# Token attention: the denominators of the softmax from sums of two neighbouring key blocks

## The chip, the cores and the metric

The kernel runs on one core of a Trainium2 chip. The metric is device time in microseconds (us) from one execution of the whole program; several runs are made and their median is used. The engines are named as in the profile: PE is TensorE (PEld its weight loads), DVE is VectorE, ACT is ScalarE, POOL is GpSimd, SP is SyncE with its DMA queue.

## What is computed

The program is a chain of three layers on a tensor of 4 images, 256 channels, 32 by 32 pixels: a convolutional attention, a block of token attention with a gated feed-forward layer, and a mixture of experts, with norms between them. The change is in the second layer alone. There each of the 4 batches has 1024 tokens, 8 heads of 32 channels, and computes

```
q2 = jnp.sum(q * q, axis=-1)
k2 = jnp.sum(k * k, axis=-1)
qk = jnp.einsum('bhqd,bhkd->bhqk', q, k)
attn = -(q2[..., :, None] + k2[..., None, :] - 2.0 * qk) / math.sqrt(hd)
attn = jnp.where(causal, attn, -jnp.inf)
attn = jax.nn.softmax(attn, axis=-1)
out = jnp.einsum('bhqk,bhkd->bhqd', attn, v)
```

The softmax is taken without subtracting a maximum: the kernel forms exp(score), multiplies it with v for the numerator and with a matrix of ones for the denominator, and divides at the end.

## The kernel before, in words

`token_block` holds the second layer. Each engine has its own program, written out by hand in order, and semaphores link them. For one batch the attention has 4 rounds: (head group 0, first 512 queries), (head group 1, first 512), (head group 0, last 512), (head group 1, last 512). A head group is 4 heads. A round walks over the key blocks of 128 keys that its queries may see: 4 in rounds 0 and 1, 8 in rounds 2 and 3. One round and one key block (kb) are a step; a batch has NS = 24 steps, numbered m. The last 4 key blocks of each round lie on the diagonal, and there only queries from `first_query(m)` on are computed, so that these four steps are 512, 384, 256 and 128 queries wide; the others are 512 wide.

One step has three stages. PE computes the scores of 4 heads in two halves of two heads (`scores`, lines 844 and 847, the second being the mask of a diagonal block), each half in its own pair of PSUM banks. ACT takes exp of each half into `probs` (line 1103), which has two slots, m % 2. PE then runs `weigh` (line 870): the numerator, v times probs, 4 heads side by side in four column groups of the array, and the denominator, ones times probs, in the same way. Both are fp32 and the trace shows 8 matmul records for each of the two. PE's order is scores(m+1), weigh(m), scores(m+2), weigh(m+1) and so on, so each scores call is queued behind the weigh of two steps earlier. A half of the scores waits until ACT has emptied its pair of banks, that is for exp of the same half one step earlier.

DVE's program in the attention (`attention`, line 1411) is a list by step. At kb == 1 of rounds 1 to 3 it runs `normalise` of the round before: a reciprocal of the denominators (line 1507) and a product (line 1509). At kb == 3 it runs `low_part` of the round before (line 1515). In the last round, at key block 5, it runs `statistics` of the next batch (lines 1275 to 1289), and at the last step `norm_factors` (line 1294) and `second_norm` (line 1475). ACT's program (line 1094) has, between the exps: at kb == 2 of rounds 1 to 3, after the exp of that step, `aT` of the round before (line 1153), a copy that waits for `normalise`; two `x_copy` pairs; and after the exp of step 22 `late_roots` and `norm_roots` (lines 1125 and 1036), square roots of which the second waits for `statistics` and which are enclosed by two table loads. All of ACT's and DVE's instructions run strictly in this order. PE's last work of the attention is weigh(23), and then `late` begins with `h2_turned` (line 909), transposes of what `second_norm` wrote.

Batches 0, 1 and 2 each carry such work for the next batch (x_turned, x_copy, statistics, norm_factors); batch 3 does not.

## Time and profile before

| what | value |
| --- | --- |
| median of 3 runs | 1603.47 us (1595.92 to 1610.03) |
| the profiled execution | 1605.05 us |
| span from its first to its last instruction | 1603.3 us |
| mean granted TensorE clock over the span | 0.896 |
| busy over the span | PE 79%, DVE 49%, ACT 44%, POOL 26% |

The span is read as layers in order of time: the first layer until about 350 us, the token block until about 998 us, then routing and experts. The shares of busy time are means over layers with different limits, so the attention's own stretches have to be looked at. In the rows below a granted clock of 1.00 is 2.4 GHz and 0.50 is 1.2 GHz. A row of a timeline can merge several instructions of one line; its duration is then from the first start to the last end. The end of a matmul is modelled and overlaps the start of the next one.

### The profile page before, as it was taken

Reading aid. Unit: us, or ns where it says so; the run is one execution under the profiler, and the core shown is the slowest. Engines: PE = TensorE matmul, PEld = TensorE weight load, DVE = VectorE, ACT = ScalarE, POOL = GpSimd, SP = SyncE. Lnnn points to the kernel's source line nnn. Section 1 sums busy time; section 2 is a strip of 40 time slices with the busy share of each in tenths; the row PEclk is TensorE's granted clock in tenths of the full one; section 3 lists DMA queues with packets and bytes.
Section 4 is the critical chain, followed back from the end, with each engine's and each line's share of the span. In section 5 each row is a group of like instructions: output and inputs, shape, how many; then the busy total and the mean of one; then the engine's idle time right before and its main releaser. Section 6 shows DMA issues by size and latency. Waiting matters only on the chain. (4 is left out here: it accounts for less than half of the span.)

```text
span 1603.3 us, 27663 instructions
## 1 busy us (share of the span) xinstructions
PE 1267.5 (79%) x9241; PEld 905.8 (56%) x9242; DVE 786.6 (49%) x1442; ACT 697.5 (44%) x1314; POOL 412.3 (26%) x307
## 2 busy tenths in 40 slices
PE   4999999956398789779977986622299999999993
PEld 3777777743134433434444334512288888888882
DVE  3857574715545553654366343824054444444441
ACT  3444433315566756666675562311133333333321
POOL 3939393700000000000000000256223332233321
PEclk7999999977699989988998998555599999999996
DMA  5949494920600060025004201997333333333326
GB/s 178 339 140 328 165 326 147 298 92 33 108 12 14 14 132 15 1 46 101 15 1 83 50 1 53 244 273 167 73 51 54 46 49 49 53 53 51 45 38 220
DMA packets 284049, 166.64 MB, mean 104 GB/s; under 512 B 203456, under 2 KB 266176, under 8 KB 283840
## 3 DMA queue, kind: packets, MB, share of 16 engines
q1 hardware_dynamic: 268512, 142.51, 34.5%
q0 software_dynamic: 15456, 23.08, 8.0%
q8 instruction: 47, 0.77, 0.2%
q14 instruction: 34, 0.28, 0.1%
HBM read 38.66 MB, written 83.11 MB: 76 GB/s over the span
## 5 line engine op out<-in xcount | busy, mean ns | idle before, releaser
L2031 PE MATMUL moe_hbank<-moe_xT,l_w1T 128*128 128x256 f16 x1872 | 213.2, 275 | 49.9 <-DMA moe_xT<-rows_scratch 49.9
L2072 ACT ACTIVATE moe_hid<-moe_hbank,moe_b1T 128x256 f32<-128x256 f32 x312 | 130.8, 470 | 267.1 <-PE moe_hbank L2031 267.1
L2031 PEld LDWEIGHTS moe_hbank<-moe_xT,l_w1T 128*128 x1872 | 184.3, 99 | 72.5 <-issue 50.0
L2046 PE MATMUL moe_ybank<-l_w2T,moe_hid_hi 128*128 x1248 | 206.4, 273 | 0.0
L2010 POOL DMA_INDIRECT acc_scratch<-moe_y,moe_meta x78 | 121.9, 1562 | 315.6 <-DVE moe_y L2099 292.5
L1103 ACT ACTIVATE block_probs<-block_bank 128x1024 f32<-128x1024 f32 (+1 forms) x192 | 144.9, 809 | 80.2 <-PE block_bank L847 65.5
L2046 PE MATMUL moe_ybank<-l_w2T,moe_hid_lo 128*128 x624 | 170.1, 273 | 0.0
L2084 DVE TENSOR_SCALAR moe_hid_hi<-moe_hid 128x2048 f16<-128x2048 f32 x39 | 47.8, 1227 | 218.6 <-ACT moe_hid L2072 218.6
L720 POOL COPY block_stack<-block_stack 128x512 f16<-128x512 f16 x16 | 11.2, 700 | 516.7 <-ACT block_stack L1087 516.7
L2046 PEld LDWEIGHTS moe_ybank<-l_w2T,moe_hid_hi 128*128 128x128 f16 x1248 | 122.1, 98 | 14.1
L844 PE MATMUL block_bank<-block_qkT 128*128 128x512 f16 (+3 forms) x384 | 94.9, 336 | 39.3 <-DMA block_qkT<-block_stack 27.9
L363 POOL TENSOR_SCALAR conv_raw<-conv_raw 128x1024 f32<-128x1024 f32 x32 | 95.2, 2975 | 32.7 <-DMA conv_raw<-in_L_ffn_w 32.7
L844 PEld LDWEIGHTS block_bank<-block_qkT 128*128 128x128 f16 x384 | 34.1, 99 | 117.5 <-ACT block_probs L1103 62.8
L2086 DVE SCALAR_TENSOR_TENSOR moe_hid_lo<-moe_hid,moe_hid_hi 128x2048 f16<-128x2048 f32 x39 | 89.4, 2292 | 1.3
L870 PE MATMUL block_bank<-block_probs,block_v 128*32 128x512 f32 (+3 forms) x768 | 85.1, 516 | 5.8 <-ACT block_probs L1103 5.8
L369 POOL TENSOR_TENSOR conv_raw_lo<-conv_raw,conv_raw_hi 128x1024 f16<-128x1024 f32 x32 | 69.0, 2157 | 74.0 <-DMA w_parts<-conv_raw_lo 71.6
L269 PE MATMUL block_bank<-block_qkv,block_hT 128*128 128x256 f16 (+1 forms) x384 | 70.6, 334 | 20.9 <-ACT block_qk L1062 8.3
L870 PE MATMUL block_bank<-block_probs,block_ones 128*32 128x512 f32 (+3 forms) x768 | 81.4, 496 | 0.0
L269 PE MATMUL block_bank<-block_down,block_ff_hi 128*128 128x256 f16 x256 | 51.7, 307 | 24.2 <-DVE block_ff_lo L1491 24.2
L1507 DVE RECIPROCAL block_h<-block_bank 128x512 f32<-128x512 f32 x12 | 40.3, 3357 | 61.5 <-PE block_bank L870 61.3
L474 ACT ACTIVATE conv_pt_hi<-conv_turned 128x1024 fp32r<-128x1024 f32 x32 | 32.9, 1028 | 82.1 <-PE conv_turned L412 82.1
L269 PEld LDWEIGHTS block_bank<-block_qkv,block_hT 128*128 128x128 f16 x384 | 36.0, 99 | 55.7 <-issue 12.2
(348 smaller groups left out, 2611.0 us busy)
## 6 DMA issues: line engine op xcount, KB each, us to landing
rows_scratch<-l_blank SPq DMA_DIRECT2D x32, 1056.0 KB, 7.5
conv_raw<-in_L_ffn_w SPq DMA_DIRECT2D x32, 512.0 KB, 4.9
w_parts<-conv_raw_lo SPq DMA_DIRECT2D x32, 256.0 KB, 3.4
w_parts<-conv_raw_hi SPq DMA_DIRECT2D x32, 256.0 KB, 3.6
l_xs<-in_x SPq DMA_DIRECT2D x8, 512.0 KB, 6.9
x_scratch<-l_xs SPq DMA_DIRECT2D x4, 1024.0 KB, 4.0
block_xin<-x_scratch SPq DMA_DIRECT2D x16, 256.0 KB, 3.1
acc_scratch<-block_res SPq DMA_DIRECT2D x16, 256.0 KB, 2.2
```

The source lines that it names most:

```text
L269: last = pe.matmul(out, a, b, start=start and k == 0, stop=stop and k == n - 1)
L363: pool.tensor_scalar(raw[q][:, :], raw[q][:, :], GAIN, None, ALU.mult).then_inc(raw_scaled, 1)
L369: pool.tensor_tensor(raw_lo[:, :], raw[q][:, :], raw_hi[q][:, :], ALU.subtract).then_inc(raw_lo_done, 1)
L844: last = pe.matmul(bank[:, 2 * (n % 2) + i, q0:512], qkT[:, 1, hh, kb * P:(kb + 1) * P], qkT[:, 0, hh, qh * 512 + q0:(qh + 1) * 512], star ...
L870: last = pe.matmul(out[i * HD:(i + 1) * HD, q0:512], lhs, probs[:, m % 2, i, q0:512], start=kb == 0, stop=kb == last_kb)
L1103: act.activation(probs[:, m % 2, 2 * p:2 * p + 2, q0:512], src, ACT.Exp, scale=SCALE).then_inc(S["exp_done"], 1)
L2010: pool.indirect_dma_start(acc, bass.IndirectOffsetOnAxis(ap=meta[r][:, t, 0:1].bitcast(U32), axis=0), y[r % 2][:, t, :], None, compute_op= ...
L2031: last = pe.matmul(hbank[:, c, :], w1T[:, e, wp, k, c * P:(c + 1) * P], xT[q][:, xp * CC + k, :], start=n == 0, stop=n == 5)
L2046: last = pe.matmul(ybank[q][:, t, :], (hid_hi, hid_lo)[hp][q][:, c, t * P:(t + 1) * P], w2T[:, e, wp, c, :], start=n == 0, stop=n == 3 * H ...
L2072: act.activation(hid[q][:, c, :], hbank[:, c, :], ACT.Gelu, bias=b1T[:, e, c:c + 1], scale=1.0 / (GAIN * GAIN)).then_inc(S["gelu_done"], 1)
L2084: dve.tensor_scalar(hid_hi[q][:, :, :], hid[q][:, :, :], HID_GAIN, None, ALU.mult).then_inc(S["hi_done"], 1)
L2086: dve.scalar_tensor_tensor(hid_lo[q][:, :, :], hid[q][:, :, :], HID_GAIN, hid_hi[q][:, :, :], ALU.mult, ALU.subtract).then_inc(S["lo_done" ...
```

## The change

`probs` gets four slots (m % 4) instead of two. `weigh` keeps only the numerator. Key blocks 2k and 2k+1 of a round form a couple. DVE gets `couple`: once exp of both steps is done and the numerator of the even step has been computed, it adds the probabilities of the odd step onto those of the even step in place, over the columns that the odd step has (4 heads times its width). PE gets `lengths(k)`: the four products with ones on the sum, one set per couple instead of one per step, queued after the numerator of step 2k+2, the first step of the next couple. ACT's exp now waits for the numerator of four steps ago and for the denominator of the couple that used its slot. `normalise` and `last_round` also wait for the denominators. In DVE's list `couple` stands ahead of everything else of its step.

```diff
--- before.py
+++ after.py
@@ -609,6 +609,7 @@
     steps = [(r, kb) for r, (_, qh) in enumerate(rounds) for kb in range(4 * (qh + 1))]
     diagonal = [kb >= 4 * rounds[r][1] for r, kb in steps]
     NR, NS = len(rounds), len(steps)
+    SLOTS, COUPLES = 4, NS // 2
 
 
     O_STEP, X_STEP, ROOT_STEP = steps.index((NR - 2, 4)), steps.index((NR - 1, 2)), NS - 2
@@ -632,7 +633,7 @@
 
         stack = s.sb("stack", [P, 2, 2, 2, H, 4, HD], F16)
         qkT = s.sb("qkT", [P, 2, H, T], F16)
-        probs = s.sb("probs", [P, 2, 4, 512])
+        probs = s.sb("probs", [P, SLOTS, 4, 512])
         ff_hi, ff_lo = s.sb("ff_hi", [P, FC, 512], F16), s.sb("ff_lo", [P, FC, 512], F16)
         n1, n2 = s.sb("n1", [P, D]), s.sb("n2", [P, D])
         later, barrier = s.sb("later", [P, P], F16), s.sb("barrier", [P, P], F16)
@@ -666,7 +667,7 @@
                  "w_full", "w_hi", "w_lo", "half_inv", "half_attn", "half_hi", "half_lo", "consts", "xin0", "xin1", "norm_loaded", "x_full", "x_copied", "stats_done", "front_scal", "front_act", "late_scal", "late_act", "res_done", "u_done", "h_done",
                  "hsq_done", "h_full", "hT_hi", "hT_lo", "qkv_full", "qk_copied", "v_copied", "gsq_done", "fac_done",
                  "scaled", "squared", "summed", "stack_hi", "stack_dup", "stack_lo", "stack_x", "turned0", "turned1",
-                 "score_full", "exp_done", "av_step", "inv_done", "attn_done", "aT_hi", "aT_lo",
+                 "score_full", "exp_done", "av_step", "coupled", "den_done", "inv_done", "attn_done", "aT_hi", "aT_lo",
                  "o_full", "x2_done", "x2sq_done", "h2_done", "h2_full", "h2T_hi", "h2T_lo", "gate_full", "silu_done", "ffprod_done",
                  "ff_hi_done", "ff_lo_done", "down_full", "o_added", "t2_done", "t2_stored", "log_done", "alpha_done", "passed")
         S = {n: s.sem(n) for n in names}
@@ -862,14 +863,24 @@
                             pe.wait_ge(S["attn_done"], b * NR + (r - 1))
                         if kb == 0 and r == NR - 1:
                             pe.wait_ge(S["o_added"], b * PAIRS + 2)
-                        num, den = bank[:, 4 + 2 * (r % 2), :], bank[:, 5 + 2 * (r % 2), :]
-                        for out, own in ((num, True), (den, False)):
-                            for i in range(4):
-                                hh = 4 * hg + i
-                                lhs = v[:, kb, hh * HD:(hh + 1) * HD] if own else ones[:, :]
-                                last = pe.matmul(out[i * HD:(i + 1) * HD, q0:512], lhs, probs[:, m % 2, i, q0:512],
-                                                 start=kb == 0, stop=kb == last_kb)
+                        num = bank[:, 4 + 2 * (r % 2), :]
+                        for i in range(4):
+                            hh = 4 * hg + i
+                            last = pe.matmul(num[i * HD:(i + 1) * HD, q0:512], v[:, kb, hh * HD:(hh + 1) * HD], probs[:, m % SLOTS, i, q0:512],
+                                             start=kb == 0, stop=kb == last_kb)
                         last.then_inc(S["av_step"], 1)
+
+                    def lengths(k):
+
+                        m = 2 * k
+                        r, kb = steps[m]
+                        q0 = first_query(m)
+                        den = bank[:, 5 + 2 * (r % 2), :]
+                        pe.wait_ge(S["coupled"], b * COUPLES + k + 1)
+                        for i in range(4):
+                            last = pe.matmul(den[i * HD:(i + 1) * HD, q0:512], ones[:, :], probs[:, m % SLOTS, i, q0:512],
+                                             start=kb == 0, stop=kb == 4 * (rounds[r][1] + 1) - 2)
+                        last.then_inc(S["den_done"], 1)
 
                     scores(0)
                     for m in range(NS):
@@ -879,12 +890,15 @@
                             x_turned(nb, 0)
                             x_turned(nb, 1)
                         weigh(m)
+                        if m % 2 == 0 and m:
+                            lengths(m // 2 - 1)
                         if m == O_STEP:
                             output(b, 0)
                             output(b, 1)
                         if m == X_STEP + 1 and nb is not None:
                             x_turned(nb, 2)
                             x_turned(nb, 3)
+                    lengths(COUPLES - 1)
 
                 def output(b, pr, nb=None):
                     wh, wl = w["o"]
@@ -1095,12 +1109,13 @@
 
                     for m in range(NS):
                         q0 = first_query(m)
-                        act.wait_ge(S["av_step"], b * NS + max(m - 1, 0))
+                        act.wait_ge(S["av_step"], b * NS + max(m - SLOTS + 1, 0))
+                        act.wait_ge(S["den_done"], b * COUPLES + max((m - SLOTS) // 2 + 1, 0))
                         for p in range(2):
                             n = 2 * m + p
                             act.wait_ge(S["score_full"], b * 2 * NS + n + 1)
                             src = bank[:, 2 * (n % 2):2 * (n % 2) + 2, q0:512]
-                            act.activation(probs[:, m % 2, 2 * p:2 * p + 2, q0:512], src, ACT.Exp, scale=SCALE).then_inc(S["exp_done"], 1)
+                            act.activation(probs[:, m % SLOTS, 2 * p:2 * p + 2, q0:512], src, ACT.Exp, scale=SCALE).then_inc(S["exp_done"], 1)
                         if steps[m][1] == 2 and steps[m][0] > 0:
                             aT(b, steps[m][0] - 1)
                         if nb is not None and m in (X_STEP + 1, X_STEP + 2):
@@ -1411,6 +1426,8 @@
                 def attention(b, nb):
                     for m in range(NS):
                         r, kb = steps[m]
+                        if kb % 2:
+                            couple(b, m // 2)
                         if kb == 1 and r > 0:
                             normalise(b, r - 1)
                         if kb == 3 and r > 0:
@@ -1428,11 +1445,21 @@
                                 norm_factors(nb)
                             second_norm(b, 0)
 
+                def couple(b, k):
+
+                    m = 2 * k
+                    cols = slice(first_query(m + 1), 512)
+                    dve.wait_ge(S["exp_done"], b * 2 * NS + 2 * (m + 2))
+                    dve.wait_ge(S["av_step"], b * NS + m + 1)
+                    both = probs[:, m % SLOTS, :, cols]
+                    dve.tensor_tensor(both, both, probs[:, (m + 1) % SLOTS, :, cols], ALU.add).then_inc(S["coupled"], 1)
+
                 def last_round(b):
 
                     hg, qh = rounds[NR - 1]
                     r = NR - 1
                     dve.wait_ge(S["av_step"], b * NS + NS)
+                    dve.wait_ge(S["den_done"], (b + 1) * COUPLES)
                     for half, (inv_sem, attn_sem) in enumerate((("half_inv", "half_attn"), ("inv_done", "attn_done"))):
                         cols = slice(half * 256, (half + 1) * 256)
                         inv = h[:, 4 + 2 * (r % 2) + half, :]
@@ -1502,6 +1529,7 @@
                     hg, qh = rounds[r]
                     m = max(i for i in range(NS) if steps[i][0] == r)
                     dve.wait_ge(S["av_step"], b * NS + m + 1)
+                    dve.wait_ge(S["den_done"], b * COUPLES + (m + 1) // 2)
                     inv = h[:, 4 + 2 * (r % 2):6 + 2 * (r % 2), :].rearrange("p a b -> p (a b)")
                     num, den = bank[:, 4 + 2 * (r % 2), :], bank[:, 5 + 2 * (r % 2), :]
                     dve.reciprocal(inv, den).then_inc(S["inv_done"], 1)
```

## Rows read from the trace of the kernel before

**Rows 1.** Windows, batches 2 and 3: length, busy PE PEld DVE ACT POOL, clock, DMA
```profile
732.80:798.00 65.20, 61.91 (x579) 24.75 (x576) 25.47 (x44) 44.30 (x67) 0.00 (x0) 0.97 0.18 39
883.50:946.20 62.70, 59.66 (x561) 22.59 (x558) 21.13 (x23) 40.80 (x61) 0.00 (x0) 0.97 0.12 27
```

**Rows 2.** Groups of instructions by line in the attention of batch 2
```profile
L1103 ACT ACTIVATE block_probs<-block_bank 128x1024 f32<-128x1024 f32 (+3 forms) x48 | 36.3, 809 | 19.2 <-PE block_bank L847 15.4 <-PE block_bank L844 3.6
...
L870 PE MATMUL block_bank<-block_probs,block_ones 128*32 128x512 f32 (+3 forms) x192 | 19.9, 486 | 0.0
```

**Rows 3.** Timeline of PE in batch 2: start us, us, engine, line, operation, tiles, count
```profile
748.60 0.83 PE L870 MATMUL block_bank<-block_probs,block_ones 128*32 128x384 f32 x8
...
750.36 0.61 PE L870 MATMUL block_bank<-block_probs,block_ones 128*32 128x256 f32 x8
...
752.12 0.40 PE L870 MATMUL block_bank<-block_probs,block_ones 128*32 128x128 f32 x8
...
756.91 1.06 PE L870 MATMUL block_bank<-block_probs,block_v 128*32 128x512 f32 x8
757.79 1.04 PE L870 MATMUL block_bank<-block_probs,block_ones 128*32 128x512 f32 x8
758.76 1.04 PE L844 MATMUL block_bank<-block_qkT 128*128 128x512 f16 x4
759.73 1.06 PE L870 MATMUL block_bank<-block_probs,block_v 128*32 128x512 f32 x8
797.45 0.43 PE L870 MATMUL block_bank<-block_probs,block_v 128*32 128x128 f32 x8 [1.46 <-ACT block_probs L1103]
```

**Rows 4.** Timeline of ACT in batch 2, columns as in rows 3
```profile
747.71 1.09 ACT L1103 ACTIVATE block_probs<-block_bank 128x512 f32<-128x512 f32 x2 [1.48 <-PE block_bank L847]
...
751.55 3.77 ACT L1103 ACTIVATE block_probs<-block_bank 128x1024 f32<-128x1024 f32 x4 [1.10 <-PE block_bank L844]
756.58 1.94 ACT L1103 ACTIVATE block_probs<-block_bank 128x1024 f32<-128x1024 f32 x2 [1.26 <-PE block_bank L844]
758.40 0.63 ACT L1153 ACTIVATE block_turned_hi<-block_h 128x512 f16<-128x512 f32 x1
...
793.82 1.28 ACT L1125 ACT_TABLE_LOAD   x1
```

**Rows 5.** Timeline of DVE in batch 2
```profile
743.92 3.36 DVE L1507 RECIPROCAL block_h<-block_bank 128x512 f32<-128x512 f32 x1 [12.56 <-PE block_bank L870]
747.31 0.69 DVE L1509 TENSOR_TENSOR block_h<-block_bank,block_h 128x512 f32<-128x512 f32 x1
...
789.75 1.41 DVE L1275 BATCH_NORM_STATS2 block_stats<-block_t 128x6 f32<-128x256 f32 x4 [3.55 <-ACT block_t L1032]
791.29 0.64 DVE L1279 BATCH_NORM_AGGREGATE block_mv<-block_stats 128x2 f32<-128x6 f32 x8
...
792.61 0.17 DVE L1289 TENSOR_SCALAR block_ta<-block_td 128x8 f32<-128x8 f32 x1
795.46 0.25 DVE L1294 RECIPROCAL block_roots<-block_tb 128x16 f32<-128x16 f32 x1 [2.68 <-ACT block_tb L1036]
...
796.06 1.67 DVE L1475 SCALAR_TENSOR_TENSOR block_qk<-block_qk,block_rr,block_n 128x256 f32<-128x256 f32 x4
```

**Rows 6.** Groups of DVE instructions by shape, whole run
```profile
L2086 DVE SCALAR_TENSOR_TENSOR moe_hid_lo<-moe_hid,moe_hid_hi 128x2048 f16<-128x2048 f32 x39 | 89.4, 2292 | 1.3
L2084 DVE TENSOR_SCALAR moe_hid_hi<-moe_hid 128x2048 f16<-128x2048 f32 x39 | 47.8, 1227 | 218.6 <-ACT moe_hid L2072 218.6
...
L1454 DVE TENSOR_TENSOR block_res<-block_t,block_u 128x512 f32<-128x512 f32 x16 | 10.0, 683 | 0.0
```

**Rows 7.** Busy time by stretch at the end of the attention of batch 2, with granted clock
```profile
799.00:803.00 4.00, 2.42 (x13) 1.09 (x12) 3.62 (x5) 1.01 (x3) 0.00 (x0) 1.00 0.00 0
803.40:805.40 2.00, 0.06 (x1) 0.00 (x0) 1.82 (x4) 0.47 (x2) 0.00 (x0) 1.00 0.00 0
805.40:808.70 3.30, 3.24 (x16) 2.32 (x17) 3.30 (x10) 1.83 (x2) 0.00 (x0) 0.51 0.00 0
```

## The prediction

> **What bounds the kernel now.** I read first the page's busy shares, then windows over the attention of single batches, then the timelines of PE, ACT and DVE side by side. In the attention of batch 2 PE is busy 61.9 of 65.2 us and ACT 44.3; in batch 3, without work for a next batch, PE 59.7 of 62.7 [rows 1]. The reader is to see that PE sets the pace while ACT waits for it: 19.2 us of idle time before the exps, all released by PE's scores [rows 2]. DVE is busy only 25.5 us [rows 1], but in lumps: a reciprocal of 3.36 us per round [rows 5].
>
> A full step takes PE 2.82 us, from 756.91 to 759.73: numerator 0.88, denominator 0.97, scores 0.97 [rows 3]. A step costs ACT two exps, 1.94 us [rows 4]. The attention is a loop of three engines with little slack: exp of one half lets PE write that half's next scores, and those let ACT go on. ACT can never be more than one step ahead, whatever the number of probs slots, since the score banks hold one step.
>
> **What the change removes.** The denominators of the odd steps: widths 384 and 128 in rounds 0 and 1, and 512, 512, 384, 128 in rounds 2 and 3. The row of a group lasts 0.07 us longer than the distance to the next (1.04 against 0.97), so I take 0.97, 0.76 and 0.33 for 512, 384 and 128 columns [rows 3]. Of each, 0.09 (0.97 less 0.88) comes with the turn back to scores and stays. Removed are 0.88, 0.67 and 0.24: 2 x 0.91 + 2 x 2.67 = 7.2 us a batch, 28.6 us in all. That is the whole gain, were PE's time all that counts. An odd step then takes PE 1.94 us, no less than ACT's 1.94, and the handover of about 0.25 us comes on top, so about a quarter of the gain goes to ACT even with nothing else late.
>
> **What it adds on DVE.** The widest add has 2048 elements, 4 heads of 512. No row shows that instruction. An fp32 sum of 512 takes 0.68 us, and a two-input instruction of 2048 takes 2.29; four separate sums of 512 would be 2.73, and a one-input instruction of 2048 takes 1.23 [rows 6]. I take the two-input row less the 0.08 by which DVE's records overlap: 2.2 us, and 1.68 and 0.62 for widths 384 and 128. Ends: 1.23 and 2.73. A batch has 4 x 2.2 + 4 x 1.68 + 4 x 0.62 = 18.0 us; DVE then is at 43.5 of 65 us, so it is not the bound by its sum. Before the denominators of an ordinary couple the add is covered: between the exp that frees it and the PE instruction that needs it stand one numerator, one set of scores and one more numerator, 0.88 + 0.97 + 0.88 = 2.73 us, against 2.2 and two handovers. The waits added to ACT on slots of four steps ago come last nowhere; I take nothing for them (ends 0 and 3 us in all, 96 steps at 0.03).
>
> **What it moves, and the new wait.** In DVE's list `couple` of key blocks 0 and 1 stands ahead of `normalise` of the round before. `couple` needs the exps of key block 1, which `normalise` never needed. Before, in round 2, the reciprocal started 0.07 us after the last denominators and its product ended at 756.67, while ACT came to `aT` only at 758.40 [rows 4]. (By rows 5: 3.39 from the reciprocal's start to the product's, plus 0.69.) `normalise` was hidden with 1.8 us to spare. Now it starts after exp of key block 1 plus the add. Behind `normalise` wait ACT's `aT`, behind that the exps of key block 3, and behind them PE's numerator and its next scores.
>
> I laid the three orders beside each other on the clock of batch 2, with the durations above, handovers of 0.12 to 0.15, and exps of 1.94, 1.52, 1.09 and 0.66. The old order laid in this way ends within 0.5 us of the trace everywhere. After / before:
> - Round 1. PE is 1.2 us ahead when it starts. Exp of key block 1 ends at 744.8; add 1.68, reciprocal and product 4.1: 750.6. ACT is at `aT` at 746.9 and waits 3.7. Copy 0.6, first half of exp 0.33: the scores of round 2 start at 751.6 / 750.5, **1.1 late**.
> - Round 2. Exp of key block 1 ends 756.2, add 2.2, 4.1 more: 762.5. ACT waits from 758.8, 3.7 us. Scores of key block 4 start 764.2 / 761.2, **3.0 late**; PE has been idle 2.9 us. The rest of the round gives back 0.5 to 0.7: **2.3 late** at round 3.
> - Round 3. Exp of key block 1 ends 781.3; product 787.6; ACT waits from 783.2, 4.4 us. Scores of key block 4 at 789.4 / 785.3, **4.1 late**; at step 20 3.5 late.
> - End. In the step of key block 5 `couple` stands ahead of `statistics`. Before, half the statistics ran earlier and the rest from 789.75, beside the exps of that step [rows 5]. Now from the end of those exps at 795.8: add 1.7, all the statistics 4.3 (eight records of 0.35, aggregates 0.65, four small ones 0.85) to 801.8, `norm_roots` to 802.1, table load 1.28 [rows 4], last exp 0.66: 804.0. Behind it stands the last add, 0.6, and only then `norm_factors` and `second_norm`, of which the first transposes want half: 1.35. They start at 806.1 / 798.0, and the second pair waits 0.3 again: **8.4 late**.
>
> Batch 3 has no statistics; it is laid out to 6.0 late. Sum 3 x 8.4 + 6.0 = **31.2 us**. With adds at 1.23 us for the widest it comes to 17, at 2.73 to 39. What follows in `late` hangs on these transposes, in all engines, so it all moves on.
>
> **The clock.** The granted clock in this attention is 0.97 on average [rows 1]. A wait of 1.46 us at 797.45 leaves it at 2.4 GHz [rows 3]. After a stretch from 799 with 2.4 of 4.0 us busy and then a stretch of 2.0 us nearly empty it is 0.51, that is 1.2 GHz, for 3.3 us [rows 7]. The new waits of PE are 2.9, 2.9, 2.7 and 5 us, each longer than the 2.0. Laying half clock over the 3.4 us behind each of them costs 3.5 us a batch, 14 in all, less than half of the work since ACT sets the pace there; none costs 0. I take 2.5 a batch, **10 us**, the greater part since each wait exceeds the one that did it.
> The Trainium skill, "TensorE: Matmul & The Clock Gate", section "HAM oscillation — how this bites in real kernels", says that a kernel whose bursts of matmuls are parted by waits finds the clock throttled again at each burst. By that rule the sum would be 1650, by no fall of the clock 1636; the trace agrees for one wait [rows 7].
>
> **The sum.** 1605.05 (the profiled execution, 1603.3 of it span) + 31.2 + 10 = 1646.3. That execution stood 1.6 above the median of the runs shown; the forecast for a median is 1645.
>
> **Rivals.**
> - All new waits bring the clock down: + 31.2 + 14 - 1.6 = 1649. For: rows 7. Against: 1.46 us did not, and the phase of a wait can matter. Chance 0.2.
> - The adds are cheaper than the two-input row, or the engines recover more between the waits: + 17 and 0 to 5 of clock: 1621 to 1626. For: nothing here shows such an add. Against: the reciprocal and product, 4.1 us, stay behind the exps at any price of the add; with adds at nothing I still get + 2. Chance 0.15.
> - Gain eaten but no more: 1595 to 1612. It needs both cheap adds and `statistics` absorbed. Chance 0.06.
> - Faster: PE's 7.2 us a batch come through, 1603.5 - 28.6 x 0.75 = 1582. Its place is the full steps, its price the denominators, and it decides if ACT's `aT` doesn't wait, that is if `normalise` ends before ACT is there. For: PE is at 95% and everything else idles beside it. Against: the lay-out of round 2 misses that by 3.7 us. Chance 0.05.
> - The change doesn't shed the work (denominators as long as before for another reason): the waits without the gain, some 1665. Chance 0.04.
>
> **Chances and range.** The forecast holds 0.5. One per cent, 16 us, is about what can be told from no change. Faster by over 1%: 0.05. Within 1% (1587 to 1619.5): the eaten gain and the lower edge of the cheap adds, 0.08. Slower by over 1%: 0.87. Range: from the cheap adds with little clock, 1621, to adds at 2.73 (+ 39) with all the clock (+ 14), 1655, and a little for the spread of runs: 1620 to 1659.
>
> **What would show it.** In the changed profile: denominators with ones at half the count, 96 records a batch instead of 192, and some 11 us busy instead of 19.9 [rows 2]; an add of 2.1 to 2.3 us at its widest; ACT idle 3 to 4.5 us before each of 12 `aT` copies, released by the product at line 1509's successor; a reciprocal that starts right behind an add instead of behind the denominators; `norm_roots` waiting some 3 us for `statistics` in three batches; the attention of batch 2 some 73 to 77 us long instead of 65.2, of batch 3 68 to 73; half clock behind most of PE's long waits. Wrong would be: `aT` without a wait, PE waiting mainly for the adds of ordinary couples, or a loss that sits behind the attention, in `late`.

## The result, and the profile after

The changed kernel is slower: 1657.09 us, median of 4 runs (1647.68 to 1658.44), against 1603.74 for the kernel before beside it; ratio 1.0323, 95% interval 1.0263 to 1.0382. The profiled execution took 1655.82 us, span 1654.1, 50.8 above the profiled one of before.

First where the time went. The windows below run from the first scores of each batch to the first transposes that follow its attention; the columns are window, length, busy us (instructions) of PE, PEld, DVE, ACT and POOL, granted clock, DMA share, GB/s. Before:

```profile
427.95:496.92 68.97, 64.86 (x584) 25.62 (x585) 28.49 (x51) 46.85 (x71) 0.61 (x1) 0.94 0.24 47
579.07:646.96 67.89, 63.05 (x587) 25.14 (x584) 28.24 (x52) 46.33 (x70) 0.52 (x1) 0.97 0.19 46
731.87:798.03 66.16, 62.87 (x585) 25.32 (x585) 25.47 (x44) 45.22 (x68) 0.00 (x0) 0.97 0.20 42
880.02:946.15 66.13, 61.18 (x571) 23.37 (x568) 23.51 (x31) 43.89 (x64) 0.14 (x1) 0.97 0.18 32
sum 269.15, PE 251.97 PEld 99.45 DVE 105.70 ACT 182.28 POOL 1.28; mean PE 62.99 PEld 24.86 DVE 26.43 ACT 45.57 POOL 0.32
```

After:

```profile
430.58:512.44 81.86, 64.69 (x489) 24.05 (x489) 45.91 (x62) 46.98 (x71) 0.62 (x1) 0.85 0.20 40
595.16:676.37 81.21, 63.40 (x490) 23.70 (x488) 45.10 (x62) 46.13 (x69) 0.00 (x0) 0.88 0.16 39
761.86:841.83 79.97, 63.21 (x488) 23.62 (x489) 42.90 (x55) 45.70 (x68) 0.00 (x0) 0.87 0.16 36
923.76:998.12 74.36, 58.31 (x475) 20.43 (x472) 41.79 (x42) 44.76 (x66) 0.62 (x1) 0.93 0.14 30
sum 317.40, PE 249.60 PEld 91.79 DVE 175.71 ACT 183.58 POOL 1.23; mean PE 62.40 PEld 22.95 DVE 43.93 ACT 45.90 POOL 0.31
```

The attentions are 12.9, 13.3, 13.8 and 8.2 us longer: 317.4 less 269.15 is 48.2 us, nearly all of it. The stretches between them are the same to 0.6 us (579.07 less 496.92 is 82.15, 595.16 less 512.44 is 82.72). Two more readings: DVE's busy time has gone up by 70 us, and PE's has gone down by only 2.4, though a hundred instructions a batch are gone and 28.6 us of work with them. The work that is left has become slower: the clock is 0.85 to 0.93 where it was 0.94 to 0.97.

ACT in batch 2, the copies of line 1168 (1153 before, [rows 4]) and the root of line 1050:

```profile
782.52 0.63 ACT L1168 ACTIVATE block_turned_hi<-block_h 128x512 f16<-128x512 f32 x1 [3.87 <-DVE block_h L1537]
...
795.18 0.63 ACT L1168 ACTIVATE block_turned_hi<-block_h 128x512 f16<-128x512 f32 x1 [3.82 <-DVE block_h L1537]
...
821.51 0.63 ACT L1168 ACTIVATE block_turned_hi<-block_h 128x512 f16<-128x512 f32 x1 [4.60 <-DVE block_h L1537]
...
837.40 0.22 ACT L1050 ACTIVATE block_tb<-block_ta 128x16 f32<-128x16 f32 x1 [2.46 <-DVE block_ta L1304]
```

Each copy now stands behind an idle stretch of 3.8 to 4.6 us, released by the product of `normalise`. [rows 4] show none ahead of the copy at 758.40. DVE at the same places:

```profile
776.74 1.76 DVE L1455 TENSOR_TENSOR block_probs<-block_probs 128x1536 f32<-128x1536 f32 x1 [4.45 <-PE block_bank L869]
778.41 3.35 DVE L1535 RECIPROCAL block_h<-block_bank 128x512 f32<-128x512 f32 x1
...
788.86 2.29 DVE L1455 TENSOR_TENSOR block_probs<-block_probs 128x2048 f32<-128x2048 f32 x1 [1.34 <-ACT block_probs L1118]
791.07 3.35 DVE L1535 RECIPROCAL block_h<-block_bank 128x512 f32<-128x512 f32 x1
...
831.35 1.76 DVE L1455 TENSOR_TENSOR block_probs<-block_probs 128x1536 f32<-128x1536 f32 x1 [3.31 <-ACT block_probs L1118]
833.02 2.70 DVE L1290 BATCH_NORM_STATS2 block_stats<-block_t 128x6 f32<-128x256 f32 x8
...
839.70 0.69 DVE L1455 TENSOR_TENSOR block_probs<-block_probs 128x512 f32<-128x512 f32 x1 [2.34 <-ACT block_probs L1118]
```

The reader is to see the sequence add, reciprocal, with no gap: 2.21 us from the start of the widest add to the next instruction (788.86 to 791.07), and the reciprocal follows the add instead of the denominators [rows 5]. At 831.35 the add is ahead of the statistics, all eight of which then run in one piece, and ACT's root waits 2.46 us for them; at 839.70 the last add is ahead of `norm_factors`. PE's waits of over 2 us in this batch:

```profile
783.48 1.73 PE L845 MATMUL block_bank<-block_qkT 128*128 128x512 f16 x4 [2.85 <-ACT block_probs L1118]
...
796.78 0.39 PE L845 MATMUL block_bank<-block_qkT 128*128 128x512 f16 x1 [2.90 <-ACT block_probs L1118]
...
798.87 1.94 PE L869 MATMUL block_bank<-block_probs,block_v 128*32 128x512 f32 x8
...
821.53 1.76 PE L793 MATMUL block_bank<-all_ident,block_xin 128*128 128x128 f32 x7 [3.84 <-DVE block_h L1537]
...
839.63 0.65 PE L869 MATMUL block_bank<-block_probs,block_v 128*32 128x128 f32 x8 [4.24 <-ACT block_probs L1118]
```

The third of them, at 821.53, is not ahead of scores but ahead of line 793, the transposes of the next batch's input. And the numerator at 798.87, behind the second wait, lasts 1.94 us, where one of that width took 1.06 [rows 3]. The windows before and behind these waits, with the granted clock as the third number from the right:

```profile
783.40:786.80 3.40, 3.32 (x15) 0.98 (x16) 2.98 (x5) 2.24 (x4) 0.00 (x0) 0.54 0.00 0
793.90:796.70 2.80, 0.00 (x0) 0.00 (x0) 1.22 (x2) 1.52 (x3) 0.00 (x0) 1.00 0.00 0
796.70:800.20 3.50, 3.26 (x16) 0.85 (x16) 2.44 (x2) 2.92 (x4) 0.00 (x0) 0.59 0.00 0
817.30:821.50 4.20, 0.39 (x2) 0.00 (x0) 4.17 (x4) 0.00 (x0) 0.00 (x0) 0.97 0.00 0
821.50:824.90 3.40, 3.37 (x19) 1.98 (x23) 0.05 (x1) 3.39 (x5) 0.00 (x0) 0.54 0.25 73
...
839.60:843.10 3.50, 3.00 (x22) 1.60 (x23) 2.71 (x7) 0.12 (x1) 0.00 (x0) 0.50 0.00 0
```

Behind each of the four waits of batch 2 the clock is 0.50 to 0.59, that is 1.2 GHz for most of the 3.4 to 3.5 us that follow. During the second and the third wait, 793.90 to 796.70 and 817.30 to 821.50, it is at 2.4 GHz still (1.00 and 0.97).

Not every new wait does it. The whole attention has 15 of them, four in each of batches 0 to 2 and three in batch 3. Behind 12 the granted clock is 0.50 to 0.63; behind one, of 3.01 us at 945.67, it is 0.77, since it falls only about 2 us later; and behind two, of 2.46 us at 467.49 and 2.52 at 959.23, it stays at 1.00. The first of these two and the one of 3.01 us:

```profile
467.49:470.89 3.40, 3.20 (x24) 1.26 (x24) 2.50 (x2) 2.89 (x4) 0.00 (x0) 1.00 0.00 0
...
945.67:949.07 3.40, 2.99 (x16) 0.69 (x16) 3.24 (x6) 2.54 (x4) 0.00 (x0) 0.77 0.00 0
```

### The profile page after: what moved, and what is told of

Same layout as the page of the kernel before. It is cut to its first block and busy times, and to the rows that moved or that the text cites. A ratio compares the mean times of both kernels' runs of the same rounds, so it can differ in the third digit from the quotient of the medians.

```text
span 1654.1 us, 27098 instructions
## 1 busy us (share of the span) xinstructions
PE 1271.5 (77%) x8857; PEld 901.2 (54%) x8858; DVE 860.9 (52%) x1490; ACT 699.6 (42%) x1314; POOL 412.5 (25%) x307
## 5 line engine op out<-in xcount | busy, mean ns | idle before, releaser
L2112 DVE TENSOR_SCALAR moe_hid_hi<-moe_hid 128x2048 f16<-128x2048 f32 x39 | 47.9, 1228 | 216.7 <-ACT moe_hid L2100 216.7
L845 PE MATMUL block_bank<-block_qkT 128*128 128x512 f16 (+3 forms) x384 | 105.8, 363 | 67.8 <-ACT block_probs L1118 39.2
L1455 DVE TENSOR_TENSOR block_probs<-block_probs 128x1536 f32<-128x1536 f32 (+2 forms) x48 | 75.9, 1581 | 137.5 <-ACT block_probs L1118 75.0
L869 PE MATMUL block_bank<-block_probs,block_v 128*32 128x512 f32 (+3 forms) x768 | 92.9, 559 | 14.3 <-ACT block_probs L1118 14.3
L269 PE MATMUL block_bank<-block_turned_hi,block_gate 128*128 128x512 f16 x128 | 49.0, 426 | 22.2 <-DVE block_probs L1514 16.2
```

Source lines behind the costliest of these rows:

```text
L269: last = pe.matmul(out, a, b, start=start and k == 0, stop=stop and k == n - 1)
L845: last = pe.matmul(bank[:, 2 * (n % 2) + i, q0:512], qkT[:, 1, hh, kb * P:(kb + 1) * P], qkT[:, 0, hh, qh * 512 + q0:(qh + 1) * 512], star ...
L869: last = pe.matmul(num[i * HD:(i + 1) * HD, q0:512], v[:, kb, hh * HD:(hh + 1) * HD], probs[:, m % SLOTS, i, q0:512], start=kb == 0, stop= ...
L1455: dve.tensor_tensor(both, both, probs[:, (m + 1) % SLOTS, :, cols], ALU.add).then_inc(S["coupled"], 1)
```

## The experiments

They ran in later sessions, in which the kernel before takes 1591.4 to 1593.5 us; so ratios to it are compared, and the changed kernel was run there twice:

> The changed kernel itself, beside the others on one chip, as their measure: ratio to before 1.026 to 1.038 as recorded; all differences between variants are read against this run.

Measured: 1637.94, ratio 1.0287 [1.0250, 1.0324]. And once more, with more runs:

> The changed kernel once more beside the busy waits, as their measure: ratio to before 1.025 to 1.035; granted clock 0.85 to 0.89 in the attention of batches 0 to 2.

Measured: 1637.91, ratio 1.0288 [1.0264, 1.0311]. The loss in these sessions is 44 to 47 us, where it was 53 in the first.

**Thin adds.** Is it the adds' time?

```diff
-                    cols = slice(first_query(m + 1), 512)
+                    cols = slice(511, 512)
```

> The changed kernel, with each of the 48 adds cut to one column per head (4 elements); every wait, the order of all engines and the halved denominators stay. Left out of the computation: the probabilities of the odd key blocks in the denominators. Theory A (the adds' time, 18 us a batch, counts because they stand in DVE's queue ahead of the reciprocal, the statistics and the second norm): nearly all of the loss goes, 1600 to 1612 us, and waits of ACT at the copies fall from 3.9-4.6 us to under 2. Rival B (the order alone does it: the reciprocal starts only behind the exps of key block 1, whatever the add costs): at least half of the loss stays, 1630 or more. Rival C (the halved denominators would be a gain if only the adds were free): 1575 to 1590.

Measured: 1602.29, ratio 1.0048 [1.0032, 1.0064]. The loss falls from 44 us to 8 or 9. Theory A holds and B falls, but not all of A is as expected: the copies still wait 27.1 us in 12 times, 2.3 each, where under 2 was expected, since the reciprocal stays behind the exps of key block 1. C falls as well: even free adds leave no gain under this order.

**The order at key block 1.**

```diff
-                        if kb % 2:
-                            couple(b, m // 2)
                         if kb == 1 and r > 0:
                             normalise(b, r - 1)
+                        if kb % 2:
+                            couple(b, m // 2)
```

> The changed kernel with normalise ahead of couple in the step of key block 1. Theory A: the copies of ACT wait 1.2 to 2.6 us instead of 3.9 to 4.6, but PE now waits 1 to 3.4 us for the add that comes behind the reciprocal; the laid-out sum falls from 49 to 35 us over before: 1635 to 1645. Rival D (ACT's wait at the copies is nearly the whole loss, and moving it away frees it): 1615 to 1625. Rival E (the half clock and PE's lack of work behind any stall make it all the same): no change within 5 us of 1656.

Measured: 1624.59, ratio 1.0185 [1.0155, 1.0216], 30 to 32 us above before. The expectation was written against 1604: by ratio A is 1.019 to 1.026 and D 1.007 to 1.013, so the measured one lies at A's lower edge, though 1624.59 as an absolute time would fall into D. The waits moved as expected. Who waited for whom, total us, times, longest:

```profile
DVE block_h L1535 <- PE block_bank L881: 52.7, 12, 5.0
...
PE block_bank L881 <- DVE block_probs L1455: 24.6, 12, 3.3
...
ACT block_turned_hi L1168 <- DVE block_h L1537: 23.8, 12, 2.6
```

The copies wait 23.8 instead of 48.3 us, and 24.6 us of PE waiting for sums have come in their place; 16 us net, by the difference of the ratios. D and E fall. The line at the top shows the third place of a queue: the reciprocal now waits for the denominators of the last, narrow couple, which PE computes only in the step after the round. The 52.7 us are no loss by themselves (the reciprocal waited 61.3 us before the change as well, 10 times); what counts is how late it starts, and that is measured below.

**The order at the end of the attention.**

```diff
-                        if kb % 2:
+                        if kb % 2 and m not in (X_STEP + 3, ROOT_STEP + 1):
                             couple(b, m // 2)
...
                             second_norm(b, 0)
+                        if kb % 2 and m in (X_STEP + 3, ROOT_STEP + 1):
+                            couple(b, m // 2)
```

> The changed kernel with the adds of steps 20/21 behind statistics, and that of steps 22/23 behind norm_factors and second_norm. Theory A: the stretch from step 20 to the first transposes of late gets 3 us shorter in three batches and 1 in the last; with the half clock behind it 8 to 13 us in all: 1643 to 1649. Rival: the end of the attention is not part of it (the statistics only move), 1653 to 1658.

Measured: 1628.67, ratio 1.0217 [1.0182, 1.0253]. By ratio that is about 11 us below the changed kernel, within the 8 to 13 expected; the absolute times of the expectation went by the first session, and as ratios to 1604 they would be 1.024 to 1.028, above the measured one. In the attention the root of line 1050 waited 7.2 us for the statistics in the changed kernel, in 3 times; in this run it doesn't wait for them.

**Both orders.**

> The changed kernel with both moves in DVE's queue: normalise ahead of couple at key block 1, and statistics, norm_factors and second_norm ahead of the couples of their steps. Theory A: the two gains (20 and 16 us) act at different places of a batch and add up, less a little: 15 to 25 us above before, ratio 1.009 to 1.016; what is left are PE's waits for the add behind the reciprocal. Rival (one wait takes the other's place, so the moves don't add): 28 us or more above before.

Measured: 1614.57, ratio 1.0146 [1.0106, 1.0186]: 21 to 23 above before. The single moves took away 16 and 11, both together 22: they add up, less a little, within the uncertainty of 6 to 9 us that each of these differences has. Left over, as expected:

```profile
DVE block_h L1537 <- PE block_bank L881: 52.1, 12, 5.0
...
PE block_bank L881 <- DVE block_probs L1457: 25.7, 13, 3.3
ACT block_turned_hi L1168 <- DVE block_h L1539: 23.8, 12, 2.6
```

**The cost without the gain.**

```diff
+    SINGLE = (0, 1, 2, 3, 4, 5, 6, 7, 8, 9, 10, 11)
...
+                        if m // 2 in SINGLE:
+                            own_lengths(m)
...
-                    dve.tensor_tensor(both, both, probs[:, (m + 1) % SLOTS, :, cols], ALU.add).then_inc(S["coupled"], 1)
+                    dve.tensor_tensor(sums[:, :, cols], both, probs[:, (m + 1) % SLOTS, :, cols], ALU.add).then_inc(S["coupled"], 1)
```

> The changed kernel with the denominators of every step as before (two sets per couple, from the single probabilities) while DVE still does all 48 adds at the same places, into a scratch buffer that nobody reads but whose slots ACT waits for, and each add waits for the one before it. The change's cost without its gain. Theory A: PE has its 7.2 us a batch back, of which the waits hide about half: 10 to 16 us above the changed kernel, that is 4.0% to 4.4% above before. Rival F (the denominators' time is hidden entirely under the new waits): within 4 us of the changed kernel. Rival G (the loss comes from PE waiting for the sums, not from the queue order): near the kernel before, less than 1% above it.

Measured: 1651.09, ratio 1.0358 [1.0323, 1.0393], 13 us above the changed kernel beside it (11 by the ratios). That is within the 10 to 16 us of A, but 3.6% above before and not the 4.0 to 4.4% into which the expectation had translated them. So of the 28.6 us of removed denominators 11 to 13 arrive even there, and 58 us (1651.09 less 1593.47) are what the adds and their waits cost. F and G fall.

**The wait that the lay-out had missed.**

```diff
-                        if m == X_STEP and nb is not None:
+                        if m == X_STEP + 1 and nb is not None:
                             x_turned(nb, 0)
...
-                        if nb is not None and m in (X_STEP + 1, X_STEP + 2):
-                            for pr in (2 * (m - X_STEP) - 2, 2 * (m - X_STEP) - 1):
+                        if nb is not None and m in (X_STEP + 2, X_STEP + 3):
+                            for pr in (2 * (m - X_STEP - 1) - 2, 2 * (m - X_STEP - 1) - 1):
```

> The changed kernel with x_turned and x_copy of the next batch one step later, so that PE doesn't wait for the product of round 2's normalise ahead of the numerator of step 18. That wait (3.8 us of PE in each of three batches) was not in the prediction's lay-out. Theory A: the exps of step 19 stay behind the copy, so only what PE could not do meanwhile comes back: 2 to 4 us below the changed kernel, ratio to before 1.025 to 1.028. Rival (PE's 3.8 us are lost whole): 8 to 12 us below it, 1.021 to 1.023.

Measured: 1631.68, ratio 1.0256 [1.0219, 1.0293] against 1.0287: about 5 us less, but the intervals overlap, and this one reaches into the ranges of both theories. The trace says more: with the transposes out of the way PE's third wait in batch 2 is still 3.56 us, now ahead of the scores of step 20 and for the exps that stand behind the copy. So the 3.84 us were not an extra wait, which speaks for A. The last wait of the batch is 3.09 us where it was 4.24.

**Which pairs are worth adding.** The last two steps of a round are 256 and 128 wide: their pair saves 0.24 us of PE, and holds up the end of the round. Here they have their own denominators, at once:

```diff
+    SINGLE = (1, 3, 7, 11)
+    PAIRED = COUPLES - len(SINGLE)
...
+                        if m // 2 in SINGLE:
+                            own_lengths(m)
...
-                        if kb % 2:
-                            couple(b, m // 2)
                         if kb == 1 and r > 0:
                             normalise(b, r - 1)
+                        if kb % 2 and m // 2 not in SINGLE and m not in (X_STEP + 3, ROOT_STEP + 1):
+                            couple(b, m // 2)
...
                             second_norm(b, 0)
+                        if kb % 2 and m // 2 not in SINGLE and m in (X_STEP + 3, ROOT_STEP + 1):
+                            couple(b, m // 2)
```

> Both moves in DVE's queue, and the last couple of each round (widths 256 and 128) is not added: its two steps have their own denominators, at once behind their numerators, so that the round's denominators are complete in its last step and the reciprocal starts as early as before the change. Eight couples of twelve are left, whose removed denominators are 0.67, 0.88 and 0.88 and 0.67 us. Theory A: ACT's copies wait no more, PE waits only about 1 us for the first sum of rounds 2 and 3: 10 to 18 us below before, ratio 0.989 to 0.994. Rival (any add in DVE's queue costs more than its denominators give): at or above before.

Measured: 1573.80, ratio 0.9887 [0.9842, 0.9932]: faster than before by 18 us, and than the changed kernel by 64. Against the kernel with both orders and all twelve pairs it is 41 us faster (1614.57 less 1573.80): that is what the four narrow pairs of each batch cost there. Who waited for whom:

```profile
DVE block_h L1554 <- PE block_bank L881: 34.0, 12, 4.6
...
PE block_bank L894 <- DVE block_probs L1474: 2.7, 4, 0.7
```

No line of a copy waiting for `normalise` is left; PE waits 2.7 us in all for sums. DVE and then ACT in the second and third key block of round 2 in batch 2:

```profile
743.80 3.36 DVE L1554 RECIPROCAL block_h<-block_bank 128x512 f32<-128x512 f32 x1 [0.16 <-PE block_bank L881]
747.19 0.69 DVE L1556 TENSOR_TENSOR block_h<-block_bank,block_h 128x512 f32<-128x512 f32 x1
747.80 2.28 DVE L1474 TENSOR_TENSOR block_probs<-block_probs 128x2048 f32<-128x2048 f32 x1
751.33 2.29 DVE L1474 TENSOR_TENSOR block_probs<-block_probs 128x2048 f32<-128x2048 f32 x1 [1.25 <-ACT block_probs L1135]
```

```profile
746.93 1.94 ACT L1135 ACTIVATE block_probs<-block_bank 128x1024 f32<-128x1024 f32 x2 [0.40 <-PE block_bank L847]
748.75 0.63 ACT L1185 ACTIVATE block_turned_hi<-block_h 128x512 f16<-128x512 f32 x1
```

The order is reciprocal, product, add; the product ends at 747.88, the copy at 748.75 doesn't wait, and the widest add, still 2.28 us, falls into time in which DVE has nothing else to do. What the narrow pair did can be read from the start of the reciprocal, against the first exp of the round it stands in (round 2 of batch 2). With both orders and all pairs it starts 4.1 us after it (769.95, the exp at 765.85). With the wide pairs it is 1.0 (743.80 and 742.76), as before the change (752.59 and, in [rows 4], 751.55):

```profile
752.59 3.36 DVE L1507 RECIPROCAL block_h<-block_bank 128x512 f32<-128x512 f32 x1 [0.15 <-PE block_bank L870]
```

The same pairs with DVE's old order:

> The wide pairs alone, eight couples, but with DVE's queue in the changed kernel's order: couple ahead of normalise, statistics and second_norm. Theory A: the order is what costs, so this stays near the changed kernel, 1.024 to 1.034 of before; the copies of ACT still wait 3.5 us and more, 12 times. Rival (the four narrow couples cost the time, since their sums hold up the end of each round): most of the loss goes, below 1.010.

Measured: 1641.09, ratio 1.0306 [1.0274, 1.0339], and

```profile
ACT block_turned_hi L1185 <- DVE block_h L1554: 51.6, 12, 4.6
```

4.3 us a copy. The choice of pairs alone gives nothing (1.0306 against 1.0287), the order alone takes away half of the loss (1.0146), and only both together make a gain (0.9887). And with two pairs fewer; the edit sets `SINGLE = (1, 2, 3, 7, 8, 11)`, and couples 2 and 8 are the first of rounds 1 and 3, not of 1 and 2 as the expectation says:

> As the wide pairs with both moves (eight couples), and two couples fewer: the first couples of rounds 1 and 2, whose adds stand behind the reciprocal, have their own denominators again. Six couples of twelve are left. Theory A: what PE waits for those two sums is worth about what their denominators cost, so the time is that of the eight-couple kernel within 4 us, 0.985 to 0.992 of before. Rival (fewer adds, less gain, in proportion): 4 to 8 us above the eight-couple kernel, 0.991 to 0.994.

Measured: 1578.54, ratio 0.9893 [0.9854, 0.9932], the same as with eight pairs as far as can be told. The denominators of the two pairs are 0.67 and 0.88 us, 6.2 in all four batches; the uncertainty of the difference between the two runs is some 9 us, and the interval reaches into the rival's range. That an add right behind a reciprocal gives nothing and costs nothing is therefore not shown, only that two such pairs don't matter by more than this.

**The clock by itself.** PE is kept at work where it waits, with products whose weights are nought:

```diff
+                    def keep_busy(m, sets):
+
+                        num = bank[:, 4 + 2 * (steps[m][0] % 2), :]
+                        for _ in range(sets):
+                            for i in range(4):
+                                pe.matmul(num[i * HD:(i + 1) * HD, :], nought[:, :], v[:, 0:2, :].rearrange("p t d -> p (t d)"), start=False, stop=False)
...
                         if m == X_STEP and nb is not None:
+                            keep_busy(m, 4)
...
                             lengths(m // 2 - 1)
+                            if m in (6, 10) or (m == X_STEP and nb is None):
+                                keep_busy(m, 3)
+                            if m == ROOT_STEP and nb is not None:
+                                keep_busy(m, 4)
```

> The changed kernel with extra products on PE where it waits: weights of nought onto the numerator's bank, so that nothing changes in what is computed. Three sets of 4 (about 0.88 us a set) in round 1 and in round 2 ahead of the late scores, four ahead of x_turned in round 3, four ahead of the last numerator (in the last batch three in round 3 and none at the end). ACT's and DVE's orders and waits stay. Theory A (the half clock behind PE's waits costs 10 us and more beside the waits themselves): the granted clock in the attention rises from 0.87 to 0.95 or more, and the time falls by 8 to 16 us below the changed kernel. Rival H (the clock's fall is hidden under ACT's and DVE's pace): the clock rises as well, the time stays within 3 us or gets longer by what the extra products overrun.

Measured: 1626.14, ratio 1.0211 [1.0189, 1.0234] against 1.0288 [1.0264, 1.0311]: 11.8 us less by the medians, with 51 sets of products more to do. ACT's waits at its copies are the same in both, 47.9 and 47.8 us in 12 times, so it is not these that gave the time. Its attentions, and under them those of the changed kernel beside it:

```profile
432.25:509.92 77.67, 71.31 (x601) 26.18 (x601) 45.91 (x62) 46.93 (x71) 0.61 (x1) 0.94 0.20 42
591.49:666.39 74.90, 67.84 (x603) 25.18 (x600) 45.57 (x63) 46.15 (x70) 0.44 (x1) 1.00 0.18 43
751.45:828.25 76.80, 69.89 (x600) 25.59 (x601) 43.78 (x59) 45.56 (x68) 0.00 (x0) 0.96 0.19 41
911.97:984.21 72.24, 63.16 (x547) 22.47 (x544) 42.17 (x42) 44.93 (x66) 0.61 (x1) 0.98 0.15 31
sum 301.61, PE 272.20 PEld 99.42 DVE 177.43 ACT 183.57 POOL 1.66; mean PE 68.05 PEld 24.86 DVE 44.36 ACT 45.89 POOL 0.42
```

```profile
432.49:514.29 81.80, 64.63 (x489) 23.99 (x489) 45.91 (x62) 46.98 (x71) 0.62 (x1) 0.85 0.19 40
596.97:674.98 78.01, 60.48 (x491) 22.73 (x488) 45.05 (x62) 45.76 (x69) 0.00 (x0) 0.92 0.17 40
760.49:840.30 79.81, 63.13 (x488) 23.65 (x489) 42.90 (x55) 45.77 (x68) 0.00 (x0) 0.87 0.16 36
922.19:996.53 74.34, 58.25 (x475) 20.43 (x472) 41.81 (x42) 44.80 (x66) 0.61 (x1) 0.93 0.14 30
sum 313.96, PE 246.49 PEld 90.80 DVE 175.67 ACT 183.31 POOL 1.23; mean PE 61.62 PEld 22.70 DVE 43.92 ACT 45.83 POOL 0.31
```

The clock goes from 0.85, 0.92, 0.87, 0.93 to 0.94, 1.00, 0.96, 0.98. PE's busy time, 272.2, less 51 sets of 0.88 (44.9, an estimate from [rows 3]) is 227.3, close to the 223.4 that before's 252.0 less 28.6 would be. H falls. This is the price of PE's idle time that stands in no row of waits: 12.4 us of attention by these windows (313.96 less 301.61), at least, since in three of the batches the clock stayed below 1.

## Why the prediction was right, and where it was off

The forecast was 1645 with 1620 to 1659 as its range; measured 1657.1. Step by step:

- What bounds: right. PE and ACT are locked to one step; four slots of `probs` gave ACT no lead: in batch 2 after, every idle stretch of ACT ahead of an exp is released by PE's scores.
- What it removes: the groups are gone as counted. Of the 28.6 us 11 to 13 arrive in the changed order. The quarter that was to go to ACT anyway is not told apart from what the waits hid.
- The add: 2.29, 1.76 and 0.69 us, 2.21 from start to start for the widest against 2.2. The choice of the two-input row was right; the one-input row, 1.23, was far off.
- The moved queue: the heart of it, and shown. Predicted for batch 2 were waits of ACT of 3.7, 3.7 and 4.4 us at its copies; measured 3.87, 3.82 and 4.60. PE idle 2.9, 2.9, 2.7 and 5: measured 2.85, 2.90, 3.84, 4.24, so the third was longer and the fourth shorter than laid out. `norm_roots` 3: measured 2.46. Swapping the two places took 16 and 11 us away, swapping both and leaving out the narrow pairs made a gain of the loss.
- Its sum, 31.2 us: the kernel with PE kept at work has attentions of 301.6 us, 32.5 more than before's 269.15. So with little of the half clock the term is right, as far as two profiles of different sessions can be compared (before was profiled only in the first). By batches the difference is 8.7, 7.0, 10.6 and 6.1 us against 8.4, 8.4, 8.4 and 6.0: that the sum agrees to 1.3 us is in part luck, as errors of either sign cancel in it.
- What was overlooked in it: `x_turned` waits for `attn_done`, the product of round 2, and in PE's order it is ahead of numerator 18. That is why PE's third wait stands ahead of line 793. It is not why it was 3.84 and not 2.7 us long: moved one step later, the wait is still 3.56. Where the rest of that difference comes from stays open; the move gave some 5 us, with overlapping intervals.
- The clock, 10 us: the right mechanism, sized too low. I took 2.5 us a batch and gave all waits together at most 14. Taken away directly, in one session, it was 12.4 us in the attention and 12 in the whole, at least. In the first session it would be 15.7, the attentions' 48.2 less the waits' 32.5, but this is an estimate across two sessions: the changed kernel's own attentions were 317.4 us there and 314.0 later, most of it in batch 1, which ran at a clock of 0.88 there and 0.92 later. The time was nearest to the rival "all new waits bring the clock down", 1649, though its condition did not quite hold: two of the 15 waits left the clock up. The rule of the Trainium skill named beside that term, in "TensorE: Matmul & The Clock Gate", section "HAM oscillation — how this bites in real kernels", is what the trace shows in 13 of the 15 cases: the burst behind the wait finds the clock down, or loses it within it.
- The rest, 1657 less 1645, is then made of about 2 to 6 us of clock, 1 to 2 us of waits and 1.1 us between the attentions; some 3 us lie ahead of the token block, whose first scores came at 430.6 instead of 428.0, which the change doesn't touch. What is left of it lies inside the 11 us over which the runs of the changed kernel spread. In the later sessions there is less to explain: the loss is 44 to 47 us there against the 41.2 of the forecast's two terms.
- The lengths foretold for the attention, 73 to 77 and 68 to 73 us, were meant in the windows of [rows 1], which start 0.9 and 3.5 us behind the first scores. In such windows they are 79.0 (762.79 to 841.83) and 70.9 us (927.24 to 998.12): batch 2 is 2 us above its range, batch 3 inside. In batch 3 two of the three waits left the clock up or let it fall late.
- The other rivals. Cheaper adds: the adds were as priced, and the run with thin adds shows the end of that road, 0.5% above before: 8 to 9 us, where the prediction had 2 for adds at nothing. Faster: its stated condition, `normalise` ending before ACT is at the copy, was the right one: where it was met, with the wide pairs, the kernel became faster, by 18 us of the 24.8 that its eight pairs remove (28.6 less 16 times 0.24). Three quarters of that, the share in the rival's sum, would be 18.6.

What stays open: how the 44 us split between the adds' time and the order by itself. With thin adds 8 us are left, but that kernel has the gain of the halved denominators in it, 11 to 13 us in the one place where it was measured; so the order alone would cost about 20, an estimate. This wasn't run by itself.

## What to carry to other kernels

An engine's queue is strictly in order, so before work is added to an engine with time to spare, find for each place what is queued behind it, who waits for that, and how much slack that wait had: here 1.8 us of slack stood against an add of 2.2 and an exp that had not been waited for. New work that nobody waits for at once goes behind the old work that somebody waits for, and pairs that save little (0.24 us) are not worth the later end of a round: here four of them a batch turned a gain of 1.1% into a loss of 1.5%. Where an added wait leaves PE idle for about 3 us, price the half clock behind it too: here it was 12 us and more, over a third of the waits' own 32.5.

## What was not expected of the hardware

The length of PE's wait does not by itself tell whether the clock falls behind it. These are the new waits of PE in the attention of the changed kernel and of the run with `x_turned` later, with the granted clock over about the next 3 us, and a few of the kernel before:

- 3.09 us and longer: 0.50 to 0.67 each time.
- 3.00 and 3.01 us: 0.50 and 0.77 in the changed kernel, and 1.00 twice (ahead of 448.79 and 933.42) with `x_turned` later.
- 2.85 and 2.90 us: 0.51 to 0.64.
- 2.54 to 2.63 us, with `x_turned` later: 0.51 to 0.74; 2.46 and 2.52 us in the changed kernel: 1.00.
- Before the change, 1.93 and 1.91 us (ahead of 582.25 and 883.18, near the start of batches 1 and 3): 0.70 and 0.62; 1.46 us: 1.00 [rows 3].

Products of nought in such waits, 44.9 us of PE work (an estimate from [rows 3]) that computes nothing, made the changed kernel 12 us faster.
